# Scans of batches 2 to 4 with four states times 32 channels on the partitions

## The reference

```
xz = in_proj(x);  x, z = halves;  x = silu(conv4(x))            # 1024 channels each
dt, B, C = split(x_proj(x));  delta = softplus(dt_proj(dt) + b)
h = h * exp(delta * A) + (delta * x) * B                         # per token, 1024 channels x 16 states
y = sum over states of h * C;  y = (y + x * D) * silu(z);  out_proj(y)
quantized MLP: rounded int8 products of a 512x512 and a 512x256 weight, own weights for each sequence
experts: softmax router, top 2 of 16 (up * silu(gate), width 128), and 4 shared blocks under a sigmoid
```

## Time and profile before

| | us | share of the span |
|---|---|---|
| median of the 3 runs | 1689.95 | |
| span of the profiled execution | 1684.0 | |
| PE busy | 1428.3 | 85% |
| DVE busy | 1344.6 | 80% |
| POOL busy | 1060.6 | 63% |
| ACT busy | 801.0 | 48% |
| scans L1277, 512 instructions | 600.1 | |
| products L1289, 432 instructions | 289.3 | |
| chunks L663, 255 instructions | 598.8 | |

### The profile page before, as it was taken

The page is one execution under the profiler, slowest core; times in us unless marked ns, Lnnn a source line. Parts: engine busy times, 40 slices in busy tenths (PEclk is TensorE's granted clock), DMA queues, the critical chain, the costliest instruction groups (busy, mean ns, idle before and its releaser), DMA issues.

```text
span 1684.0 us, 19335 instructions
## 1 busy us (share of the span) xinstructions
PE 1428.3 (85%) x5368; PEld 809.6 (48%) x5376; DVE 1344.6 (80%) x2215; ACT 801.0 (48%) x1374; POOL 1060.6 (63%) x684
## 2 busy tenths in 40 slices
PE   7588679999599899999599899999599999836994
PEld 4233224444365565444265565444265665324783
DVE  4588999676899999786899999796899999784212
ACT  3666444246634565246634565245734565222141
POOL 0399898103999899402999899501999999522101
PEclk9899899999799999999799999999799999968997
DMA  3550001403446673613535674612534773700984
GB/s 119 220 187 25 1 0 38 135 28 116 192 138 184 208 237 123 212 38 105 228 118 188 207 234 142 212 38 102 231 113 153 233 235 130 250 25 20 350 334 140
DMA packets 94073, 252.13 MB, mean 150 GB/s; under 512 B 11024, under 2 KB 11152, under 8 KB 88848
## 3 DMA queue, kind: packets, MB, share of 16 engines
q1 hardware_dynamic: 86688, 229.93, 40.3%
q0 software_dynamic: 5120, 16.78, 3.1%
q10 hardware_dynamic: 2160, 4.19, 0.6%
HBM read 207.87 MB, written 42.99 MB: 149 GB/s over the span
## 4 chain that ended last, share of the span: by engine, by line
PE 54%; DVE 17%; issue 12%; ACT 8%; POOL 7%; DMA 1%; DVEq 0%; POOLq 0%; SPq 0%; ACTq 0%
PE bank L1946 10%; PE bank L1804 7%; DVE bank L1277 5%; PE bank L2072 5%; PE bank L1817 5%; PE bank L1876 4%; PE bank L1881 4%; POOL work L663 4%; PE bank L1975 3%; PE bank L1870 3%; PE bank L1967 2%; PE bank L1922 2%; DVE work L1289 2%; DVE pairs L1289 2%; PE bank L1845 2%
## 5 line engine op out<-in xcount | busy, mean ns | idle before, releaser
L663 POOL TENSOR_TENSOR work<-du,BB 128x1024 f32<-128x1024 f32 x255 | 598.8, 2357 | 5.2 <-DVE work L1553 4.4
L942 ACT ACTIVATE bank<-delta,A_sb 128x512 f32<-128x512 f32 x512 | 349.9, 690 | 460.7 <-DVE pairs L1289 246.2
L1277 DVE TENSOR_TENSOR_SCAN bank<-bank,work 128x512 f32<-128x512 f32 x432 | 522.6, 1219 | 7.8 <-POOL work L663 4.0
L1946 PEld LDWEIGHTS bank<-x3T,ew_up 128*128 128x128 f32 x1488 | 215.7, 193 | 72.5 <-issue 63.7
L1946 PE MATMUL bank<-x3T,ew_up 128*128 128x128 f32 (+1 forms) x1488 | 235.8, 304 | 5.2 <-issue 5.2
L1289 DVE TENSOR_TENSOR pairs<-bank,CB 128x512 f32<-128x512 f32 x240 | 161.0, 671 | 3.9 <-PE bank L1881 2.9
L608 POOL TENSOR_TENSOR col<-col,halfpow 128x4 f32<-128x4 f32 (+1 forms) x8 | 7.8, 973 | 208.9 <-DVE col L1429 208.9
L1876 PE MATMUL bank<-pairs,ident 128*128 128x512 f32 x160 | 91.9, 659 | 43.7 <-DVE pairs L1289 16.6
L1289 DVE TENSOR_TENSOR work<-bank,CB 128x512 f32<-128x512 f32 x192 | 128.3, 668 | 0.0
L1817 PE MATMUL bank<-xT,wst 128*128 128x512 f32 x256 | 118.8, 610 | 9.2 <-DVE ew_up L1266 7.4
L2072 PE MATMUL bank<-wst,zg 128*128 128x512 f32 x256 | 117.0, 593 | 0.9 <-DVE zg L1297 0.9
(11 more groups left out here) (259 smaller groups left out, 2493.4 us busy)
## 6 DMA issues: line engine op xcount, KB each, us to landing
ew_up<-in_exp_w SPq DMA_DIRECT2D x93, 512.0 KB, 3.7
ew_dn<-in_exp_w SPq DMA_DIRECT2D x93, 256.0 KB, 4.3
hm<-xs_dram SPq DMA_DIRECT2D x69, 256.0 KB, 4.6
ys_dram<-x3T SPq DMA_DIRECT2D x69, 256.0 KB, 4.6
wst<-in_w_in SPq DMA_DIRECT2D x64, 256.0 KB, 2.7
BB<-bc_dram SPq DMA_DIRECT2D x16, 1024.0 KB, 7.7
CB<-bc_dram SPq DMA_DIRECT2D x16, 1024.0 KB, 9.7
wst<-in_out_w SPq DMA_DIRECT2D x32, 256.0 KB, 3.0
```

What stands on the lines that cost most here:

```text
L663: nc.gpsimd.tensor_tensor(dBu[:, k % CHUNK_SLOTS, :, :], du[:, j % 2:j % 2 + 1, :].broadcast_to([P, 2, T]), BB[:, n0:n0 + 2, :], ALU.mult) ...
L942: nc.scalar.activation(R[q % RING][:, :], delta[:, j, :], ACT.Exp, scale=A_sb[:, j, n:n + 1]).then_inc(S["da_ready"], 1)
L1277: V.tensor_tensor_scan(prod[c % (2 * PAIR_SLOTS)] if on_pool(q) else R[q % RING][:, :], R[q % RING][:, :], dBu[:, c // 2 % CHUNK_SLOTS, c ...
L1946: ins = mm(gu_bank(v)[:, part * n:(part + 1) * n], w[:, part * D + k * P:part * D + (k + 1) * P], rhs, start=(k == 0), stop=(k == KD - 1))
```

## The change

Batch 1 (b = 0) keeps its layout. In batches 2 to 4 a scan instruction no longer holds 128 channels of one state, but 4 states x 32 channels: partition 32 s + i holds state 4 g + s of channel 32 q + i, with g and q from 0 to 3. The number of scans, exponentials and chunks stays the same.

- `delta` and `du` of each block must then stand four times on the partitions. SP writes both (256 KB each) to DRAM (`rep_dram`) and, once they are there, reads each back in four DMAs (`replicate`), 2 MB for each block. The rows of B and C are read as 4 states for each group of 32 partitions (`spread_rows`), 2 MB for each batch instead of 8 MB.
- The sum over states becomes a sum over partitions and over g. For every four units PE issues four multiplications of 32 columns with `fold` (four stacked 32 x 32 identities), each into its own 32 partitions of Y (`quad_sum`). `pair` is gone; POOL takes three products of eight instead of one.
- Products have 16 slots instead of 8.
- The last steps of softplus 4 to 7, the normalization of the experts' rows and the inverses move into the stage; the visits of the stage have a new table (`STAGE`); the experts-alone stage keeps the old one (`LATE`).
- The loads of the MLP's weights and of the residual at the end of a stage change places, since their tiles are in use until other moments.

```diff
+STAGE = Order(visits=tuple(9 + 13 * v // 4 for v in range(SHARED)) + tuple(39 + 3 * r for r in range(ROUTED)),
+              norm=1, inverses=3, x3=5, logits=7, logits_copy=9, route=10, rank=14, place=15, first_down=17,
+              gate_sums=10, gates=19, gate_weights=14, scatter=11, scatters=2)
+LOST_AT = {4: 0, 5: 0, 6: 1, 7: 1}
+ERROR_AT = {4: 6, 5: 6, 6: 7, 7: 7}
+LESS_AT = {4: 7, 5: 7, 6: 8, 7: 8}
...
-    return q % 8 in ((3, 7) if q < UNITS else (7,))
+    return q % 8 in ((3, 7) if q < UNITS else (2, 5, 7))
...
+def quad_at(g):
+    return 4 * g + 7
+REPLICATE_BEFORE = {j: min(i for i in range(3, ROUTED + 3) if STAGE.visits[SHARED + i - 3] >= NS * (j - 1))
+                    for j in range(4, NBLK)}
...
+            def replicate(b, j):
+                n = NBLK * (b - 1) + j
+                sp.wait_ge(S["delta_ready"], NBLK * b + j + 1)
+                sp.dma_start(rep_dram[j], delta[:, j, :]).then_inc(S["rep_out"], 16)
+                sp.wait_ge(S["du_ready"], NBLK * b + j + 1)
+                sp.dma_start(rep_dram[NBLK + j], du[:, j % 2, :]).then_inc(S["rep_out"], 16)
+                if j == 0:
+                    sp.wait_ge(S["a_ready"], TT * b)
+                    sp.wait_ge(S["q_ready"], 4 * TT * b)
+                elif j == 1:
+                    sp.wait_ge(S["lin_ps"], 2 * TT * b)
+                else:
+                    sp.wait_ge(S["da_ready"], UNITS * b + NS * (j - 1))
+                    sp.wait_ge(S["dbu_ready"], PAIRS * b + NS // 2 * (j - 1))
...
+                sp.wait_ge(S["rep_out"], 32 * (n + 1))
+                for src, dst, landed in ((rep_dram[NBLK + j], durep[j % 2], du_in), (rep_dram[j], drep[j % 2], delta_in)):
+                    for g in range(GROUPS):
+                        sp.dma_start(dst[g * ROWS:(g + 1) * ROWS, :, :],
+                                     src.rearrange("(q i) t -> i q t", q=GROUPS)).then_inc(landed, 16)
...
+                    if w == 3:
+                        replicate(be + 1, 2)
+                replicate(be + 1, 3)
...
+                    for i in range(4, NBLK):
+                        if REPLICATE_BEFORE[i] == j:
+                            replicate(be + 1, i)
...
-                    for i in range(4):
+                    for i in range(2):
                         softplus_lost(a, i)
-                    softplus_less(a, 0)
-                    du_block(a, 0)
-                    chunk(a, 0)
-                    for i in range(1, 4):
                         softplus_less(a, i)
+                        du_block(a, i)
                 if m is not None:
                     norm(2 * m + 1)
                 if a is not None:
+                    chunk(a, 0)
+                    for i in range(2, 4):
+                        softplus_lost(a, i)
+                        softplus_less(a, i)
...
+                        j = k // (NS // 2) + 1
+                        if j < NBLK and (k % (NS // 2) == 5 and j > 1 if b == 0 else k % (NS // 2) == 1 and j > 1):
+                            du_block(b, j)
...
+                def quad_sum(g):
...
+                    pe.wait_ge(S["prod_done"], dve_products(UNITS * b + 4 * g + 4))
+                    pe.wait_ge(S["pool_prod"], pool_products(UNITS * b + 4 * g + 4))
...
+                    for q in range(GROUPS):
+                        ins = mm(Y[q * ROWS:(q + 1) * ROWS, :], fold[:], slot(b, 4 * g + q), start=(part == 0),
+                                 stop=(part == GROUPS - 1), tile_position=(0, q * ROWS))
+                    ins.then_inc(S["nsum_done"], 1)
```

More of the change, by code:

```diff
@@ L9 @@
 from contextlib import ExitStack
+from dataclasses import dataclass
 import numpy as np
@@ L210, in build @@
         prod = [pairs[:, i, :] for i in range(4)] + [late_pairs[:, i, :] for i in range(4)]
+        slots = [CB[:, 12 + i, :] for i in range(4)] + [BB[:, 12 + i, :] for i in range(4)] + prod
+        Brep = BB[:, 0:4, :]
+        Crep = CB[:, 0:4, :]
+        A_first = x3T[:, 2, 0:NBLK * NS].rearrange("p (j n) -> p j n", j=NBLK)
+        drep = [BB[:, 8:12, :], BB[:, 4:8, :]]
+        durep = [CB[:, 8:12, :], CB[:, 4:8, :]]
         guwT = BB[:, 0:4, :]
@@ L328, in build @@
         ys_out = [sem(f"ys_out{i}") for i in range(2)]
-        bcast = [sem(f"bcast{i}") for i in range(4)]
+        spread = [sem(f"spread{i}") for i in range(4)]
+        b_in, c_in, delta_in, du_in = spread
         late_in = [sem(f"late_in{i}") for i in range(LATE_RING)]
@@ L1009, in y_rows @@
                     nc.scalar.copy(ys[n % 2], down_ps[1][:, :]).then_inc(S["y_ready"], 1)
-                if experts:
-                    for i in range(KD if scan else KD // 2):
-                        x3(i)
-                    logits_copy()
+                at = STAGE if scan else LATE
                 for p in range(UNITS + TAIL):
@@ L1017, in scan_stage @@
                         decay(b, p + 2)
+                    if scan and experts:
+                        if p in (at.norm, at.norm + 1):
+                            row_norm(b - 1, 2 * b - 1, 2 * (p - at.norm), 2 * (p - at.norm) + 2)
+                        if p in (at.inverses, at.inverses + 1):
+                            inverses(b, range(4 + 2 * (p - at.inverses), 6 + 2 * (p - at.inverses)))
+                    if experts:
+                        for i in range(KD if scan else KD // 2):
+                            if p == at.x3 + (i // 2 if scan else 0):
+                                x3(i)
+                        if p == at.logits_copy:
+                            logits_copy()
                     if scan and p % NS == SKIP_AT and p // NS < NBLK:
@@ L1610, in between @@
                     one_more(a, i)
-                for i in range(4, 8):
-                    lost(a, i)
             def last(m):
@@ L2000, in scan_stage @@
                     for m in range(PAIRS):
-                        if scan and nsum_at(m) == p:
+                        if scan and b == 0 and nsum_at(m) == p:
                             nsum(m)
+                    for g in range(QUADS):
+                        if scan and b > 0 and quad_at(g) == p:
+                            quad_sum(g)
                     if scan:
```

344 lines of the change are left out of this document (215 added, 129 removed).

## The result

The changed kernel takes 1901.0 us (median; 1891.1 to 1902.7) where the kernel before takes 1689.5: a ratio of 1.124, 95% interval 1.120 to 1.127. The forecast was 1671 us in a range of 1634 to 1722. It failed in its sign, and the loss is larger than any rival gave (1764). The profiled execution of the changed kernel has a span of 1900.9 us, 216.9 more than before.

A forecast was written before the change was run, and what follows sets the result against it. DVE was taken to set the pace (29.1 us a block), POOL and PE close behind. Stages gave -8.2, -8.2 and -2.7, together -19.1: span 1665, with 5.95 around it 1671 us; range 1634 to 1722.

The forecast's parts named there:

- any rival gave (1764): Narrow multiplications on PE run one after another, 3.64 us a sum, 31 us a stage more: 1764 us; chance 0.14.
- Floors of DVE and POOL, 27.7 us a block: Five blocks among routed tiles: floors 26.7 (DVE) and 26.9 (POOL), plus 0.8 for lockstep: 27.7 each, 138.5 for five.
- Copies, "1.0 each, 4 us; the ends are 0 and 5" a stage: SP's list at blocks 4 to 7: PE waits up to 3.7 us at each copy, charged 1.0 each.
- "the bytes alone ... still fit": DMA in the five blocks: copies' 2.5 MB plus experts' 6.8 MB, 9.3 MB a block, fit in 27 us.
- one or two positions of slack: PE at the copies: its slack to DVE hides most of one wait, with 1.0 us a block to make up.
- The rival that the copies block SP: SP's list, blocks 3 to 7: PE waits the full 3.7 us and its clock falls, 45 to 60 us more; chance 0.27.
- Quad sum, 2.35 us: PE's four narrow multiplications overlap in part, five slots of 0.43 plus 0.2: 2.35 us; ends 1.2 and 3.64.
- The third rival (all side by side, about 1.2): PE's four narrow multiplications run fully side by side, about 1.2 us a sum: 1642 us; chance 0.23.
- the end of -5 against -0.9: Tail of the stage: four narrow sums on PE save 0.9 us; ends -5 and +3.
- that rival's "copies cost nothing": Five blocks, all side by side: POOL the only bound, PE catches up, copies free, 136 us; chance 0.23.
- Shared blocks, +4.1 (ends 0 and +10): Stretch of shared blocks and first rows: +3.1 us for PE's sum, +1.0 for the rest.
- Start, 0 (ends -3 and +5): Start of the stage: first scan 1.8 us later, but effects cancel by the first closing product, 0.

The follow-up runs named there:

- e1: The changed kernel without the copies of blocks 2 to 7 of each batch (scans read what blocks 0 and 1 left): 1712.9 us.
- e9: e8 with the reads of blocks 2 to 7 bringing only a sixteenth of the bytes, issues and waits kept: 1675.6 us.
- e4: The changed kernel with the copies of blocks 2 to 7 reading back a sixteenth of the bytes, all waits and issues kept: 1820.7 us.
- e8: The changed kernel with copies spread over SP's order, four error products first on POOL, and down weights two tiles ahead: 1757.0 us.
- e6: The changed kernel without copies of blocks 2 to 7, with four error products first on POOL and down weights two tiles ahead: 1674.2 us.
- e3: The changed kernel with SP loading the shared blocks' down weights two tiles ahead, not three, behind the up weights: 1850.4 us.
- e5: The changed kernel with copies written earlier, read back two to four DMAs at a time between loads, and du formed earlier: 1801.3 us.
- e2: The changed kernel with the error products of softplus blocks 2 and 3 on POOL ahead of the norm and first chunk: 1875.6 us.
- e10: e8 with the row norm of the experts' input back on ACT ahead of the stage: 1755.9 us.
- e11: e6 with the row norm of the experts' input back on ACT ahead of the stage: 1675.5 us.
- e12: e8 with the reads of blocks 2 to 7 bringing half of the bytes: 1696.0 us.

## Why the forecast was wrong, step by step

*Floors of DVE and POOL, 27.7 us a block: right.* 27.4 in the first of the changed kernel's five blocks (566 to 593 us), in which the first copy begins only at 585 us; 138.5 us for five in e1, 137.8 in e9.

*Copies, "1.0 each, 4 us; the ends are 0 and 5" a stage: this step failed.* e1 puts them at 188 us in all, 63 a stage. Three things were missing. First, SP's hold was right (8.9 us for 8.3), but the wait behind it was 9.6 us on average, not 3.7, since the rows land behind the copy's own 2 MB; with a sixteenth of these bytes (e4) it was 4.3. Second, "the bytes alone ... still fit" does not follow from the rows that it names: two reads of 1 MB in 9.7 us make 45 us for the 9.3 MB of a block, not 27. Rows 1 say the same less harshly: 172 GB/s at a DMA share of 0.54 is some 319 GB/s at a share of 1 (an estimate), and 9.3 MB in 27 us is 344. Measured, DMA is 0.95 busy in e8, and 81 us of the cost are bytes even when nothing blocks. Third, I let one or two positions of slack hide most of a wait. PE could make a delay up: with the sum at its measured 1.00 us its block is 16.4 + 4.0 + 0.9 = 21.3 us. DVE and POOL could not, with floors of 26.7 and 26.9 us in a block of 27.4 to 27.7, so what they idle behind PE is lost: the four blocks behind a copy take 7 to 14 us more than the first. The rival that the copies block SP had the right place and the falling clock; at 45 to 60 us its price was a quarter to a third of 188.

*Quad sum, 2.35 us: wrong, 1.00.* The third rival (all side by side, about 1.2) was nearest; the 0.2 us that all three prices add for the narrow form came from no row, and eight narrow instructions take only 0.14 more than two full ones. The effect came out in the tail, 21.1 us against my 25.8 (the end of -5 against -0.9), and in the shared stretch once nothing else waits: the forecast's own sum with 1.00 for 2.35 gives 25.4 + 4.0 + 0.9 = 30.3 us, and e6 has 30.1 to 30.3. But that rival's "copies cost nothing" did not follow from a PE with time to spare.

*Shared blocks, +4.1 (ends 0 and +10): wrong, +22.* Without the copies (e1) 20.6 of the 22 are gone. With them e3 brings the stretch down by 7.4, e5 by 16.7 (38.1), and e8, with both, to 35.9. I looked for POOL's scatters and PE's sums there, not at SP, where the copy of block 2 holds the down weights and these the up weights. One row of PE in the changed kernel shows the price of such an order, 13.68 us at once:

```profile
537.29 3.78 PE L2115 MATMUL bank<-x3T,ew_up 128*128 128x256 f32 x8 [13.68 <-DMA ew_up<-in_exp_w]
```

*Start, 0 (ends -3 and +5): wrong, +23.* The copies of blocks 2 to 7 have little part in it: 192.4 us in e1 for 193.8. I put the first scan 1.8 us later; it comes at 442.68 us, 10.1 later (1.2 of them from ahead of the stage). What I counted in favour (one error product instead of four ahead of `du`) was the fault: the other three went behind a chunk that waits for the copy, and ACT and then POOL waited on that. e2 and e3 take back 7 and 6 of the 23. In e6 and e9, with both, 11 to 15 us a stage are left. e10 and e11 show that it isn't the place of the row norm.

The trace of e8 says where they lie. Of its 10.9 us in the second stage 5.4 are there at the first scan already (122.1 us after the last closing product, 116.7 before). Timeline of POOL and ACT, e8:

```profile
433.49 2.34 POOL L799 TENSOR_TENSOR work<-BB,CB 128x1024 f32<-128x1024 f32 x1 [5.20 <-DMA CB<-rep_dram]
```

```profile
438.14 1.91 ACT L1095 ACTIVATE bank<-BB,A_sb 128x512 f32<-128x512 f32 x3 [9.71 <-DMA BB<-rep_dram]
```

POOL's first chunk waits for the copy of `du` of block 0 and ACT's first exponential for that of `delta`, whose reads land 6.5 to 8.5 us after their issue where the forecast had 4.6. No run leaves out the copies of blocks 0 and 1, so their price is not measured. Behind the first scan DVE idles 4.14 us until POOL's second chunk is there (from 447.87 on, done 2.3 us later), and this one stands behind a softplus step of blocks 4 to 7 that waits for ACT. Timeline of POOL and of DVE, e8:

```profile
442.07 5.83 POOL L755 TENSOR_TENSOR delta<-delta,x3T 128x512 f32<-128x512 f32 x4 [3.80 <-ACT x3T L1059]
447.87 9.27 POOL L799 TENSOR_TENSOR work<-BB,CB 128x1024 f32<-128x1024 f32 x4
```

```profile
450.31 1.22 DVE L1459 TENSOR_TENSOR_SCAN CB<-bank,work 128x512 f32<-128x512 f32 x1 [4.14 <-issue]
```

That points at the softplus steps inside the stage for this part. A kernel with them back in their old place was not run, so how the rest of the start divides stays open.

*The sum.* Without copies and with both orders the kernel takes 1674 us. The forecast without its 12 us or so for copies was 1659, 15 less. In e11, the same kernel but for the row norm, the starts are 13 to 16 us a stage too long, the shared stretch (30.1 to 30.4 us) and the tail (21.1 to 22.6) together 10 to 11 us a stage better than forecast, and some 7 us more lie behind the last closing product (232.4 us to the end, 225.0 before), which the forecast left unchanged. So that the gap is small is in part luck: some 50 us too little and some 35 us too much, against each other. The rest of the 230 us between 1671 and 1901 went with the copies and the two orders.

No version run with all the work beats the kernel before. e12 says what it would need: reading back half of the bytes would draw nearly level (+0.4%), and without any copy of blocks 2 to 7 these orders give e6's 0.9%.

## What to carry to other kernels

Work that is moved from an engine to the DMAs is not off the path because the bytes seem to fit: add the share of DMA in the stretch (0.62 here) to what the new bytes take, and expect loads to come later before it reaches 1 (at 0.85 in e12 20 us of the kernel were gone). A chain of write, wait and read in the list of the engine that issues all loads costs what stands behind it the chain's length and the bytes queued ahead of the next load (8.9 us of hold, and waits of 9.6 on average here); split it and put other loads between its parts (100 us here). And where an instruction that waits for something new is put into an engine's list, read first who waits for each one behind it.

## What was not expected of the hardware

- Four column tiles of 32, fp32 at 512 moving columns, eight instructions: 1.00 us at full clock for all, 0.14 more than one full multiplication of two instructions.
- DMA was 0.95 busy at a mean of 266 GB/s (e8, 534 to 680 us), while single slices of 3.65 us reached 409. The Trainium skill, "Perfetto Trace Analysis", section on the roofline, gives some 435 GB/s for the sixteen engines of one core. By that figure the 38.9 MB of this window would take 89 of its 146 us (an estimate from that page); the measured share says that there was hardly room left. Here the measured share decides.
- The cost of bytes is not in proportion: from a DMA share of 0.78 to one of 0.85 (e9, e12) it is 20 us of the kernel, from 0.85 to 0.95 (e8) another 61.
